# A two-layer graph network on one core: unit headers between the products, four build places, and rows reloaded before the layer ends

## The reference, cut to what matters

```
N, E, D, K, L = 6250, 106250 edges (sorted by dst), 256, 4, 2
z = h = relu(layernorm(x))
for l in range(L):
    weights  = softmax(z @ envW[l] + envb[l])                 # N x 4
    agg      = segment_sum(z[src], dst) / max(count, 1)        # mean of the neighbours' rows
    outputs  = einsum([agg, z], W[l]) + z                      # 4 experts, 512 -> 256
    z        = relu(einsum(weights, outputs))
out = x + z
```

## Time and profile before

| what | us |
|---|---|
| median of three runs | 2248.65 |
| profiled execution | 2239.89 |
| its span | 2238.0 |
| layer 0, first tail to last | 139.4 to 1246.8 |
| PE idle between the layers | 1246.8 to 1301.5 |
| layer 1 | 1301.5 to 2238.0 |
| PE busy / POOL busy in the span | 1809.5 / 1400.7 |

### The profile page before, as it was taken

The page is one execution under the profiler, slowest core; times in us unless marked ns, Lnnn a source line. Parts: engine busy times, 40 slices in busy tenths (PEclk is TensorE's granted clock), DMA queues, the critical chain, the costliest instruction groups (busy, mean ns, idle before and its releaser), DMA issues. The chain is left out here.

```text
span 2238.0 us, 42330 instructions
## 1 busy us (share of the span) xinstructions
PE 1809.5 (81%) x10188; PEld 1151.4 (51%) x10189; DVE 958.9 (43%) x2623; ACT 295.2 (13%) x728; POOL 1400.7 (63%) x1451
## 2 busy tenths in 40 slices
PE   0178888788897888978889158998999999999998
PEld 0045546445464464645545035556666565656555
DVE  6655453544545445355453223333334343333332
ACT  7211111111111111111111000000000000000000
POOL 4677574764647547476571357777777776777771
PEclk9999999999998899999999689999999999999999
DMA  7556454653545535456462676666666666666662
GB/s 228 191 159 188 145 162 124 170 177 111 151 136 163 162 110 169 133 161 182 112 172 73 214 245 177 190 179 197 180 194 182 193 187 190 182 196 180 194 179 83
DMA packets 166672, 375.99 MB, mean 168 GB/s; under 512 B 40733, under 2 KB 96598, under 8 KB 164182
## 3 DMA queue, kind: packets, MB, share of 16 engines
q0 software_dynamic: 90112, 276.91, 43.8%
q10 hardware_dynamic: 37656, 62.59, 7.8%
q1 hardware_dynamic: 38590, 32.31, 4.6%
HBM read 326.03 MB, written 44.94 MB: 166 GB/s over the span
## 5 line engine op out<-in xcount | busy, mean ns | idle before, releaser
L665 POOL DMA_INDIRECT ring<-zp_dram,gather_idx x1376 | 1327.6, 965 | 735.2 <-POOLq L87 372.0
L1118 PE MATMUL mix_ps<-w_sb,turned 128*128 128x512 f32 x1568 | 764.0, 629 | 0.0
L1050 PE MATMUL agg_ps<-ring,onehot 128*128 x3440 | 633.1, 280 | 1.3 <-issue 1.2
L1044 PE MATMUL agg_ps<-ring,onehot 128*128 x1720 | 482.0, 280 | 149.4 <-PEq L87 143.6
L1118 PEld LDWEIGHTS mix_ps<-w_sb,turned 128*128 128x128 f32 x1568 | 300.7, 200 | 299.1 <-issue 294.5
L1050 PEld LDWEIGHTS agg_ps<-ring,onehot 128*128 128x128 bf16 x3440 | 335.0, 97 | 105.7 <-issue 27.1
L724 DVE TENSOR_TENSOR onehot<-nodes,dst_t 128x512 bf16<-128x512 f32 x430 | 272.1, 693 | 115.4 <-issue 115.4
L818 DVE SCALAR_TENSOR_TENSOR mix<-mix_ps,wts,mix 128x256 f32<-128x256 f32 x392 | 189.4, 483 | 299.3 <-DVEq L87 270.5
L1044 PEld LDWEIGHTS agg_ps<-ring,onehot 128*128 128x128 bf16 x1720 | 169.1, 98 | 241.4 <-issue 208.7
L1075 PE MATMUL agg_ps<-zp,counts_sb 128*128 128x256 bf16 x1568 | 260.3, 272 | 0.0
L1072 PE MATMUL agg_ps<-zp,counts_sb 128*128 128x257 bf16 x784 | 213.1, 272 | 4.7 <-PEq L87 4.7
(11 more groups left out here) (134 smaller groups left out, 819.9 us busy)
## 6 DMA issues: line engine op xcount, KB each, us to landing
ring<-zp_dram,gather_idx POOLq DMA_INDIRECT x1376, 3.3
counts_sb<-a_dram ACTq DMA_DIRECT2D x9, 1568.0 KB, 10.0
a_dram<-counts_sb ACTq DMA_DIRECT2D x8, 1568.0 KB, 6.4
zp_dram<-zp SPq DMA_DIRECT2D x7, 1344.0 KB, 5.6
zp_dram<-parts ACTq DMA_DIRECT2D x49, 192.0 KB
zp<-zp_dram SPq DMA_DIRECT2D x7, 1344.0 KB, 22.3
z_dram<-z_out ACTq DMA_DIRECT2D x49, 128.0 KB
z_in<-z_dram ACTq DMA_DIRECT2D x49, 128.0 KB
```

The costliest lines, as they stand in the source:

```text
L665: pool.indirect_dma_start(out=ring[:, k, t, 0:3 * D], out_offset=None, in_=zp_dram[l], in_offset=bass.IndirectOffsetOnAxis(ap=gather_idx[: ...
L1044: mm = pe.matmul(agg_ps[:, bank, 0:D + 1], onehot[:, h, place, t, :], rows[:, :, 2 * D:3 * D + 1], start=place == 0 and t == 0, stop=True, ...
L1050: mm = pe.matmul(agg_ps[:, bank, 0:D], onehot[:, h, place, t, :], rows[:, :, part * D:(part + 1) * D], start=False, stop=True, skip_group_ ...
L1118: mm = pe.matmul(mix_ps[i][:, :], turned[:, what, c, :], w[:, i * HALF:(i + 1) * HALF], start=n == 0, stop=n == 3)
```

## The change

- SP reloads five of the seven groups of `zp` in the last round of layer 0, once the dense sum has read the old rows and the new rows of the earlier rounds are stored; ACT issues the weights and the last two groups when the layer is over (before: all by SP, then).
- The header of the next sparse sum is read during the tail, between its products. Units 0 to 3 stand in a row for four or more units (`head_units`), with another copy for fewer, which is jumped over; units 4 and 5 have a test each; the loop begins with the seventh.
- Build places: four instead of two, so DVE writes the first keys of all four windows ahead of the mean; more trips of any window follow after the softmax (`other_keys`). PE's windows stand one product later, and their counts are read one slot earlier.
- ACT moves window 0 between exp and the scaling of z; the split of a block's parts is one step later on DVE, and so are the stores on ACT.

```diff
-        s_bready = [sem(f"build_places{p}_ready") for p in range(2)]
-        s_bfree = [sem(f"build_places{p}_free") for p in range(2)]
+        s_ohf = [sem(f"other_onehots{h}_free") for h in range(2)]
+        s_bready = [sem(f"build_places{j}_ready") for j in range(GROUP)]
+        s_bfree = [sem(f"build_places{j}_free") for j in range(GROUP)]
...
+STRAIGHT, PLACES = 4, 6
+def head_units(eng, n, use, between):
+    with eng.If(n >= STRAIGHT):
+        for i in range(STRAIGHT):
+            use(i)
+            if i == 1:
+                between()
+    with eng.Else():
+        use(0)
+        for i in range(1, STRAIGHT - 1):
+            with eng.If(n > i):
+                use(i)
+        between()
+def more_units(eng, n, use):
+    for i in range(STRAIGHT, PLACES):
+        with eng.If(n > i):
+            use(i)
+def reload_rows(eng, g):
+    a, b = xrange(g)
+    eng.dma_start(zp[:, a:b, 0:3 * D], zp_dram[1][a * P:b * P, :].rearrange(
...
             if l:
+                with sp.Fori(0, rounds_of(sp)) as _:
+                    take(sp, s_zkept)
+                    take(sp, s_zused)
+                for g in range(XG - 2):
+                    reload_rows(sp, g)
                 sp.wait_ge(s_z1[1], 1)
                 for h in range(2):
                     take(sp, s_idx[0][h], 16)
                     sp.dma_start(gather_idx[:, h * half:(h + 1) * half],
                                  src_t[:, h * half:(h + 1) * half]).then_inc(s_idx[l][h], 16)
-                for c in range(CC):
-                    sp.dma_start(w_sb[:, c, :, :], W[l, :, c * P:(c + 1) * P, :].rearrange(
-                        "k p o -> p k o")).then_inc(s_w[l], 16)
-                for g in range(XG):
-                    a, b = xrange(g)
-                    sp.dma_start(zp[:, a:b, 0:3 * D],
...
-            other_units(dve, dve.snap(others_from[h]), dve.snap(others_to[h]),
-                        lambda u, place: compare(h, u, place).then_inc(s_ohr, 1))
+            start, end = dve.snap(others_from[h]), dve.snap(others_to[h])
+            with dve.If(start < end):
+                with dve.Fori(start, end) as u:
...
             settle(nc.vector.tensor_scalar(nodes[:, h, :], node0[:], block_base[:, bass.ds(blk, 1)], None,
                                            ALU.add))
             lo, hi = units_of(dve, blk)
-            start = dve.snap(first_units(dve, lo, hi, lambda u, place: compare(h, u, place)))
-            next_units(dve, start, hi, lambda u, place: compare(h, u, place))
+            n = dve.snap(hi - lo)
+            def use(i):
+                if i:
+                    compare(h, unit_no(lo + i), i)
+            head_units(dve, n, use, lambda: None)
+            more_units(dve, n, use)
             compare(h, lo, 0).then_inc(s_ohset, 1)
-            more_units(dve, start, hi, lambda u, place: compare(h, u, place).then_inc(s_ohr, 1))
-            dve.reg_mov(others_from[h], start + 4)
+            dve.reg_mov(others_from[h], lo + PLACES)
             dve.reg_mov(others_to[h], hi)
-        def window_keys(dn, g, j):
...
+            w, lo, hi = window_tiles(dn, g, j)
+            tile_keys(w, j, lo)
+        def other_keys(dn, g, j):
+            w, lo, hi = window_tiles(dn, g, j)
             with dve.If(lo + 2 < hi):
                 with dve.Fori(lo + 2, hi, 2) as t:
-                    trip(nc.s_assert_within(t, 0, TILES - 1,
-                                            skip_runtime_bounds_check_because="below hi"))
+                    tile_keys(w, j, nc.s_assert_within(t, 0, TILES - 1,
...
                         with dve.If(r + 1 < rounds):
                             compare_block(sparse_block(dve, r, PER_ROUND + 1), 1)
                     build = first and k < NG
+                    if first and k:
+                        split()
                     if build:
-                        window_keys(dn, k, 0)
+                        for j in range(GROUP):
+                            first_keys(dn, k, j)
                     take_mean((k + 1) % 2)
-                    softmax(l)
-                    if build:
-                        for j in range(1, GROUP):
-                            window_keys(dn, k, j)
+                    if first and k == PER_ROUND - 1:
+                        dve.sem_inc(s_zused, 1)
+                    take_logits(l)
                     if first:
                         keep_z(block_of(dve, r, dn, k + 1), (k + 1) % 2)
+                    take_weights()
+                    if build:
+                        for j in range(GROUP):
+                            other_keys(dn, k, j)
                     combine(l)
-            softmax(l)
-            combine(l)
+                if first:
+                    split()
+            def last():
+                take_logits(l)
+                take_weights()
+                combine(l)
+                if first:
+                    split()
...
-        def finish(l, blk):
+        def begin(l):
             if l < L - 1:
                 take(act, s_over)
                 take(act, s_zfs, 16)
                 take(act, s_hls, 16)
                 nc.scalar.activation(z_out[:], mix[:], ACT.Relu)
                 nc.scalar.activation(parts[:, 0:D], mix[:], ACT.Relu).then_inc(s_hi, 1)
...
+                for c in range(CC):
+                    act.dma_start(w_sb[:, c, :, :], W[l, :, c * P:(c + 1) * P, :].rearrange(
+                        "k p o -> p k o")).then_inc(s_w[l], 16)
+                for g in range(XG - 2, XG):
+                    reload_rows(act, g)
                 take(act, s_ast, 16)
...
+                    if first and k:
+                        finish(l, block_of(act, r, dn, k - 1))
                     if not first and k == PER_ROUND:
                         load_counts(dn1)
-                    weigh(l, k % 2)
                     if first and k < NG:
-                        move_windows(dn, k)
+                        weigh(l, k % 2, lambda: move_windows(dn, k, (0,)))
+                        move_windows(dn, k, (1, 2, 3))
                         if k == NG - 1:
                             act.sem_inc(s_built, 1)
-                    finish(l, blk)
+                    else:
+                        weigh(l, k % 2)
+                    begin(l)
+                    if not first or k == ORDER - 1:
+                        finish(l, blk)
+                    if first and k == 0:
+                        act.sem_inc(s_zkept, 1)
...
+        def header(blk, into):
+            def bounds():
+                into["lo"], into["hi"] = units_of(pe, blk)
+            def count():
+                into["n"] = pe.snap(into["hi"] - into["lo"])
+                into["at"] = [pe.snap(into["lo"] % RU)]
+            def places(a, b):
+                for i in range(a, b):
+                    into["at"].append(pe.snap((into["lo"] + i) % RU))
+            return [bounds, count, lambda: places(1, 3), lambda: places(3, PLACES)]
...
-            lo, hi = units_of(pe, blk)
+                if place == PLACES:
+                    mm.then_inc(s_ohf[h], 1)
+            def add_unit(i):
+                add(head["at"][i], i)
             take(pe, s_ohset)
-            add_unit(lo, 0)
-            start = pe.snap(first_units(pe, lo, hi, add_unit))
-            between()
-            next_units(pe, start, hi, add_unit)
-            more_units(pe, start, hi, add_unit)
-            other_units(pe, pe.snap(start + 4), hi, add_unit)
+            head_units(pe, head["n"], add_unit, between)
+            more_units(pe, head["n"], add_unit)
+            with pe.If(head["n"] > PLACES):
+                with pe.Fori(head["lo"] + PLACES, head["hi"]) as u:
+                    add(pe.snap(unit_no(u) % RU), PLACES)
...
+            window_at = {1: 0, 3: 1, 4: 2, 5: 3}
+            next_at = {0: 0, 1: 1, 3: 2, 4: 3}
+            step_at = {2: 1, 6: 3} if build else {0: 1, 2: 1, 4: 1, 6: 1}
...
+                        mm.then_inc(s_half[i], 1)
+                    place = 4 * i + n
+                    if build and place in window_at:
+                        summed = window(window_at[place], tiles)
+                    if build and place in next_at:
+                        tiles = window_tiles(*build, next_at[place])
+                    for _ in range(step_at.get(place, 0)):
+                        if steps:
+                            steps.pop(0)()
...
                 dn = dense_no(pe, r)
+                head = whole_header(block_of(pe, r, dn, 1))
...
-                    tail(l, (dn, k) if first and k < NG else None, True)
+                    into, steps = {}, ()
+                    if k < ORDER - 1 and k + 2 != PER_ROUND:
+                        steps = header(block_of(pe, r, dn, k + 2), into)
+                    tail(l, (dn, k) if first and k < NG else None, True, steps)
+                    head = into
```

155 lines of the change are left out of this document (70 added, 85 removed).

## The result

The changed kernel takes 2224.07 us (median of 4 runs, 2221.49 to 2230.41) against 2248.93 for the kernel before in the same set: a ratio of 0.9898, interval [0.9871, 0.9924]. It is faster, by 25 us and not by 84. The profiled execution has a span of 2219.7 us (before 2238.0).

What follows compares the result with a forecast made beforehand. PE's stream was taken as the spine, stretched by the gap, layer 0 waits and small breaks. 2239.9 - 15 - 50 - 8 - 10 = 2157, plus 8.8 for the median: 2166, rounded to 2165; range 2105 to 2240.

Steps and rivals of the forecast that it cites:

- The gap: Between the layers: index loads no longer wait behind the reloads, POOL's 14.66 us stall goes; -15 us, bounds 0 and -35.
- The build tails: Layer 0, k = 0 to 3: PE's waits for window keys shrink, DVE's pass sets the pace; -65, less 15 for hand-overs, -50 us.
- PE's start near 1266: Gap: PE starts with the first landed unit, near 1266 and not 1301, 35 us earlier, which isn't itself the gain.
- the 11 further trips over 32 tails cost about 2.5 each: Layer 0 build steps: each further trip costs a key set and PE's wait, 0.8 us in the mean, giving a 22.1 us pass.
- `win_ps` under 60 us: Sign for the build steps: PE's wait before its windows' products falls from 114.0 to under 60 us.
- Headers and branches: PE's sparse sums: parity test and register steps go; -8 us in layer 0 outside build steps, -10 in layer 1.
- half of it, since the gathers pace part of them: Layer 1: its 41 sparse sums gain half of the 0.5 us counted per sum in layer 0, -10 us together.
- after a far jump: PE's idle time at a round's start, 2.68 us, used to price the jump over the second copy at up to +150.
- The slow rival: Jump over the second copy, behind the fourth unit, costs 2.0 us in each of 57 sums, +114; total 2298, chance 0.10.
- Rival 4: Gap: semaphores release the early reloads late, SP still busy at 1255, PE starts late; 2180, inside the likeliest range, no own chance.
- Rival 1: Layer 0: DVE takes all of that layer's gain through a longer pass; total 2225, chance 0.16.
- Rival 2: More gain: layer 1 runs into the gathers' floor, at most -54, and layer 0's passes take 20.5; 2100, chance 0.08.

Runs made afterwards that it cites:

- e1: The kernel before with only the early reload of `zp` on SP (all but two groups), the last two groups and weights on ACT; 0.9938 of the kernel before.
- e4: The changed kernel with further trips of windows 0 and 1 written among the first keys, ahead of the mean, window numbers kept in registers; median 8 to 11 us lower.
- e9: The changed kernel with one-hots behind the weights (k = 0 to 2), the plan's numbers kept in registers, window 0's further trips right behind the logits; 0.967 of the kernel before.
- e11: The changed kernel with the window's numbers read once and kept in registers for the further trips, nothing else moved; 27 us off the changed kernel's control run.
- c_after: The changed kernel run again, unaltered, as control for the other runs; 0.989 of the kernel before.
- e6: The changed kernel with four more small PE products in each of layer 1's 49 tails; layer 1 took 918.1 and 916.1 us.
- e8: The changed kernel without the straight run of units: each unit behind the first has its own branch, no second copy is jumped over; 2224.7 us.
- e7: The changed kernel with 36 of 49 chunks of each dense sum in layer 1 left out, so its sums are wrong; 2172 us.
- e2: The changed kernel with PE's header of the next block read ahead of each sum again, not between the tail's products; 2224.6 us.
- e10: The kernel of e9 with the next block's z also written behind the one-hots in steps k = 0 to 2; 0.965 of the kernel before.

## Why the prediction was wrong

A gain of 84 us was forecast and 25 measured. The time lies inside the outer range, but by the path of none of its cases. By parts: the gap -16.5 for -15, the build tails -9.0 for -50, the rest of layer 0 -5.8 for -8, layer 1 +15.1 for -10. So 41 us are missing in the build tails and 25 in layer 1.

**The gap: right.** -15 forecast, 87.9 - 71.4 = 16.5 measured, and e1 gives 15.9 by itself. PE's start near 1266 was forecast for a first gather at 1257.87, 8 us ahead of PE; it was 11.3, and the early start bought nothing beyond POOL's stall, as argued. The early reloads did not push the last stores back.

**The build tails: mechanism half right, size wrong.** -50 forecast, 827.8 to 818.9 measured, -9. The step that failed is "the 11 further trips over 32 tails cost about 2.5 each (a set, and PE's wait for it), 0.8 in the mean". I priced a further trip by its own length and forgot where the change puts it: behind everything else of DVE's step, while PE's first window needs it first. One such wait is 7.5 to 9.2 us, in three of the ten tails, and is paid again in products at 1.2 GHz. The ten tails got 21 us longer. The forecast's parts have them about 5 shorter: 4 at k = 1 by 1.8, 3 at k = 3 by 5.1, and each of the 10 by 2.5 - 0.8 = 1.7 above the mean. That is 26 of the 41 us that this term missed. e4 took 21 back, nearly all in the three tails where the order counts, and e9 took 41.

The plain tails gave 29.9 where the rest of the sum, 65 - 5 - 15, has 45: the other 15. Their lengths came out near the forecast (22.1 and 22.6 at k = 1 and 2 for 22.1, 27.0 at k = 3 for 26.3), but I had subtracted them from means in which the longer further tails of before were counted (its plain ones took 23.0, 23.3 and 29.9). And that the lengths came out is luck, for the reason was wrong: DVE's pass is not their bound. e11 makes the pass 2.5 us shorter and the plain tails 0.3. What holds them, shown for n = 8 only, is the chain keys, mean, logits, exponential, ACT's move, window 2. It had been named ("what is left ends with ACT's move"), but not priced, and the four reads (3.3 forecast, 4.1 measured) lay beside it. Two costs of PE's were in no term: the test and the count read behind windows 0 and 2, 21.4 us of idle time, and the slower products behind a short stand (n = 8). The sign that the forecast set, `win_ps` under 60 us, failed at 95.2.

**Headers and branches: right in layer 0, wrong in layer 1.** k = 4 and 5 of layer 0: 270.2 to 264.4, -5.8 for -8. Layer 1: -10 forecast, +15.1 measured in this profile and +19.5 in c_after's. A clean interval did get shorter (k = 4: 128.7 to 121.8 over eight, -0.9 each), more than the 0.5 that were priced for a sum, or the 0.25 counted here. The failed step is "half of it, since the gathers pace part of them", which let the rest pass through to the total. It doesn't: e6 shows that 22 us more in the tails cost nothing, and e8 that 19 us less at k = 5 come back as 12 at k = 2. Only a large piece comes through, and only down to the floor of 862: e7's 98 gave 55.

What else was added comes on top: 5 us more of idle time ahead of a round's first unit (14.5 to 19.5), 8.5 of idle time without a wait behind it, and 6.3 us more of PE busy time for the same products, at a clock of 0.96 for 0.98, while POOL waits 71.5 us for a free unit instead of 57.1. The 5 us are not a wait for the one-hots. In n = 60 DVE had written them 11 us before, and what fills the idle time is the branch back to the loop's start and two reads of the plan: the first read starts at 8.42 us into the tail before, 9.05 in the changed kernel, 7.28 in e8. Of the prediction's 2.68 us "after a far jump" (that same n = 60), 1.4 us are these reads, from 8.42 to 9.82, so the row doesn't price a jump.

PE reaches the end of the ring sooner, stands, comes back slower, and POOL, with the ring full, stands longer behind the dense sum. That this is where the 15 us lie is shown by POOL's row; that the stands and the clock bring it about rests on the rows of the dense steps and on e6's clock. No experiment has isolated it, and e8 and e2 took away only half of it.

**The rivals.** The slow rival, the jump over the second copy, is ruled out, though not by the sign that the forecast set: eight stands of 1.6 to 4.5 us do lie behind fourth units of layer 1. In each the first product starts 0.35 us after SP has told that the fifth unit landed, and e8, which has no second copy to jump over, has ten and is no faster. Rival 4 is ruled out by the timeline. Rival 1's 2225 is what was measured, by luck: it gave layer 0 no gain, and layer 0 did gain, and layer 1 gave it back. Rival 2's floor exists and was put at most 54 us below, of which 14.66 were POOL's stall in the gap; from tail 49 on it is 37, and it worked against the change.

**What is left.** e9 and e10, at 0.967 and 0.965, beat both kernels. Their 1035 and 1038 us of layer 0 are 63 and 60 below before, where the forecast had 58 with a worse order.

## What to carry to other kernels

When a wait is removed by moving work earlier, list what the same edit moves later, and price that at the point where its consumer stands in line, not at its own length. Before an engine's cycles are counted as gain, find the floor of whatever feeds it through a ring, by leaving out a large piece of its work; in this kernel, 37 to 56 us above that floor, small savings came back as waits. Idle time ahead of an instruction with a semaphore's name on it may be the sequencer's own reads: look for them before filling it.
